# First attention stage: the norm behind the attention is applied on GpSimd, behind its spreading of k, instead of on VectorE

## The reference

```
x = x + attn(layernorm(x))       # once: windows of 64 tokens, 16 heads of 8
x = x + ffn_stack(layernorm(x))  # 6 layers: local attention (16 heads of 64,
                                 # windows of 32, rotary) and a gated feed-forward

# attn: qkv = xw @ W_qkv; q, k = layernorm over a head of 8, times gamma, plus beta
#       out = softmax(q k^T) v @ W_proj + b_proj
```

## Time and profile before

| what | value |
|---|---|
| runs of the kernel, us | 3247.95, 3230.7, 3246.5 (median 3246.5) |
| the profiled execution, us | 3239.37 |
| its span in the trace, us | 3237.6 |
| busy: PE, DVE, ACT, POOL | 96%, 86%, 79%, 82% |
| mean granted TensorE clock | 0.989 |
| the 32 executions of L366 on VectorE | 694 ns each on average, from 330 to 1353 |

### The profile page before, as it was taken

How to read it: one execution, slowest core, us unless ns; L and a number is a source line. 1 busy time by engine, 2 the same in 40 slices (tenths; PEclk the granted TensorE clock), 3 DMA queues, 4 the chain that set the end, 5 groups by cost and what they waited for, 6 DMA issues and landing times.

```text
span 3237.6 us, 123133 instructions
## 1 busy us (share of the span) xinstructions
PE 3121.0 (96%) x52802; PEld 2720.9 (84%) x52802; DVE 2769.2 (86%) x3716; ACT 2546.3 (79%) x3699; POOL 2647.6 (82%) x2646
## 2 busy tenths in 40 slices
PE   7988999999999999999999999999999999999997
PEld 4657888888888888888888888888888888888886
DVE  7978888888888888888888888888888888888884
ACT  5766788787878888787878877887878788878876
POOL 6758888887888888888888888887888888888873
PEclk9989999999999999999999999999999999999999
DMA  2001111111111111111111111111111111111111
GB/s 66 15 24 38 48 36 45 43 35 42 46 43 42 44 37 43 37 51 43 41 35 41 42 48 41 41 41 40 39 47 46 43 35 41 44 41 40 40 41 48
DMA packets 62044, 134.01 MB, mean 41 GB/s; under 512 B 11584, under 2 KB 35264, under 8 KB 61504
## 3 DMA queue, kind: packets, MB, share of 16 engines
q1 hardware_dynamic: 61504, 126.14, 13.5%
HBM read 21.27 MB, written 4.19 MB: 8 GB/s over the span
## 4 chain that ended last, share of the span: by engine, by line
PE 88%; ACT 2%; issue 2%; POOL 1%; DVE 0%; POOLq 0%; DVEq 0%
PE pair L215 71%; PE pair L218 17%; ACT qT L901 0%; ACT PT L882 0%; ACT X L920 0%; ACT X L906 0%; ACT sq L879 0%; ACT sq L891 0%; ACT VA L914 0%; ACT Sx L886 0%; POOL qk L1145 0%; POOL qk L1164 0%; DVE ss L1024 0%; DVE pair L1051 0%; DVE ts L1020 0%
## 5 line engine op out<-in xcount | busy, mean ns | idle before, releaser
L1164 POOL TENSOR_TENSOR qk<-qk,ts 128x1024 f32<-128x1024 f32 x384 | 910.5, 2383 | 70.5 <-DVE ts L1020 61.4
L1145 POOL TENSOR_TENSOR qk<-qk,rn 128x1024 f32<-128x1024 f32 x384 | 724.0, 1907 | 15.1
L1016 DVE TENSOR_TENSOR qk<-pair,tab 128x1024 f32<-128x1024 f32 x384 | 468.3, 1220 | 266.3 <-ACT sq L879 258.0
L879 ACT ACTIVATE sq<-pair 128x1024 f32<-128x1024 f32 x191 | 196.0, 1026 | 442.1 <-PE pair L215 441.9
L215 PE MATMUL pair<-wq_h,xs_h 128*128 128x512 f32 x1154 | 513.9, 445 | 2.5 <-issue 1.5
L1179 POOL TENSOR_TENSOR Sx<-Sx,rden 128x1024 f32<-128x1024 f32 x192 | 365.3, 1903 | 170.1 <-DVE rden L1096 170.1
L1020 DVE TENSOR_TENSOR ts<-pair,tab 128x1024 f32<-128x1024 f32 x384 | 466.4, 1215 | 0.0
L1024 DVE TENSOR_REDUCE ss<-sq 128x16 f32<-128x1024 f32 x384 | 464.3, 1209 | 0.0
L215 PE MATMUL pair<-wq_h,xs_l 128*128 128x512 f32 x1152 | 463.3, 402 | 0.1
L215 PE MATMUL pair<-wq_l,xs_h 128*128 128x512 f32 x1152 | 462.1, 401 | 0.6 <-issue 0.5
L218 PEld LDWEIGHTS pair<-small,qk 128*128 128x128 f32 x3072 | 350.2, 143 | 84.2 <-issue 53.0
(11 more groups left out here) (127 smaller groups left out, 6675.4 us busy)
## 6 DMA issues: line engine op xcount, KB each, us to landing
VB<-VA SPq DMA_DIRECT2D x192, 384.0 KB, 3.5
VB<-VA SPq DMA_DIRECT2D x96, 128.0 KB, 3.4
wq_raw<-wqkv SPq DMA_DIRECT2D x18, 512.0 KB, 5.1
xf<-xT SPq DMA_DIRECT2D x96, 64.0 KB, 1.9
xf<-xT SPq DMA_DIRECT2D x96, 63.8 KB, 2.0
wo_sb<-wo SPq DMA_DIRECT2D x6, 512.0 KB, 3.4
X<-x_in SPq DMA_DIRECT2D x4, 512.0 KB, 6.5
x_kept<-X SPq DMA_DIRECT2D x4, 512.0 KB, 2.7
```

Of the source, the lines that this page charges most:

```text
L879: A_.activation(sq[:, 0, :], one[:, :], ACT.Square).then_inc(S["squared"], 1)
L1016: V_.tensor_tensor(h3(qk[:, now, kind, :], DH), h3(source[:, :], DH), rep(factors[:, 2 * kind, b, :], HEADS, DH), ALU.mult)
L1145: G_.tensor_tensor(x, x, bc(rn[:, then, kind * HEADS:(kind + 1) * HEADS], HEADS, DH), ALU.mult).then_inc(S["scaled"], 1)
L1164: G_.tensor_tensor(qk[:, now, kind, :], qk[:, now, kind, :], ts[:, kind, :], ALU.add).then_inc(S["added"], 1)
```

## The change

GpSimd makes z in the same step as before, at the end of its own work on the tile pipeline, behind L406 and in front of the extra work of steps 8, 10 and 16 (step 4 comes before the first z). VectorE's instruction is gone. The operation, its operands and its semaphore `a_z` are the same. GpSimd now waits for its own `a_normed` before it, and for the transpose of z of two tiles ago. In the hand-over, the wait in front of `rest_of_x` is for z of tile 26 (step 34) in place of the spreading of the last tile.

```diff
@@ first_dve
-            i = s - 8
-            if tile(i):
-                if tile(i - 2):
-                    e.wait_ge(S["a_zT_done"], nth("a_zT_done", i - 2))
-                V_.tensor_scalar(z1[:, i % 2, :], X1[:, i, :], mv1[:, s % 2, 1, 0:1], rn1[:, s % 2, 2 * H1 + 1:2 * H1 + 2],
-                                 ALU.subtract, ALU.mult).then_inc(S["a_z"], 1)
@@ first_pool
                 last.then_inc(S["a_spread"], 1)
+            i = s - 8
+            if tile(i):
+                e.wait_ge(S["a_normed"], nth("a_normed", s))
+                if tile(i - 2):
+                    e.wait_ge(S["a_zT_done"], nth("a_zT_done", i - 2))
+                G_.tensor_scalar(z1[:, i % 2, :], X1[:, i, :], mv1[:, s % 2, 1, 0:1], rn1[:, s % 2, 2 * H1 + 1:2 * H1 + 2],
+                                 ALU.subtract, ALU.mult).then_inc(S["a_z"], 1)
 
             if s in (4, 10, 16):
@@ gpsimd
             first_stage(pool, first_pool, -1, TILES + 3)
-            pool.wait_ge(S["a_spread"], nth("a_spread", LAST))
+            pool.wait_ge(S["a_z"], nth("a_z", TILES + 2 - 8))
             rest_of_x(pool, first, 0)
```

## The result

The kernel with the change has a median of 3253.6 us (3238.9 to 3266.3, 16 runs), the kernel before one of 3246.3 us (3230.1 to 3255.4, 16 runs). The ratio is 1.0032, with a 95% interval of 1.0017 to 1.0047. By the ratio the change costs 5.5 to 15 us, most likely about 10 (the medians are 7.3 apart). The time lies inside the predicted range, but that range was 28 us wide, mostly for the spread between runs, so this says little. The loss lies inside the 0.5% called "same", but it is a loss, and about six times the 1.7 us of the forecast.

The account below looks back on a forecast made before the run. A first-stage ring over TensorE, ScalarE and GpSimd, not VectorE, was taken to set the step; 0 (regular steps) + 1.2 (steps 8, 10, 16) + 0.5 (hand-over) = +1.7 us, giving 3245 us, range 3230 to 3258.

Parts of the forecast that it names:

- the 0.5% called "same": Whole kernel: a change under about 0.5%, 16 us, counts as none; chances faster 0.03, same 0.92, slower 0.05.
- The regular steps cost and gain nothing: Steps 9, 11 to 15, 17 to 32: z hides in GpSimd's idle time, and VectorE's saving becomes waiting; cost and gain 0.
- the gap of 0.84: Regular steps: time z may take between GpSimd's spreading of k and L379 without moving anything; cover gone from 0.95.
- VectorE doesn't set the pace: Regular steps: TensorE releases VectorE; the rival that VectorE paces gave up to 10.8 us less, total 3234, chance 0.05.
- the ring over ScalarE and GpSimd: Regular step: closed chain of scores, transposes, L439, L445, L406 and scores again, taking 5.81 us, without VectorE.
- The head start of TensorE: Hand-over: last z earlier, block 1's transpose and projection 1.9 us earlier, lost in longer waits; worth 0. Rival keeping it: 0.05.
- z's price: z on GpSimd: 0.40 us, bounded by a scalar operation on 34 columns (0.227) and a same-size two-input operation (0.456).
- the prediction's 0.66: z on GpSimd at twice VectorE's 0.33, from the skill page; the sum would be 2.7 instead of 1.7 us.
- (b): Steps 8, 10 and 16, with other GpSimd work behind z: each z moves everything behind it, 3 x 0.40 = 1.2 us.
- (c): Hand-over: the last z, step 39, makes L1164 0.48 us later, and the chain behind it +0.5 us.
- a rival in the hand-over: Hand-over: TensorE's clock falls in a longer wait, two groups of eight transposes double, +2 us, total 3247; chance 0.2.
- slower: the operation is dear and outgrows the gap: Regular steps: z over 0.95 us lengthens 22 steps; chance 0.08, or 0.03 for 16 us or more (z = 1.43).

Follow-up runs that it names:

- the 28 steps without the four named: Whole kernel before, with z moved to GpSimd in all steps but 8, 10, 16 and 39: 3243.3 us against 3244.8, ratio 1.0001 [.9984, 1.0019].
- Its new order alone: One layer, kernel before with GpSimd's extra work spread, and VectorE dividing the attention's output ahead of the maxima: 773.2 us, ratio .2380 to the whole kernel before.
- the one-layer kernels: Kernels with one layer of the second stage instead of six, first stage and hand-over complete: before 773.2 us, after 784.5 us.
- The filled kernel: Changed kernel with one layer, TensorE repeating the products for v twice in steps 9, 11 and 17: 778.9 us, ratio .2402 to the whole kernel before.
- the last z alone: Kernel before with one layer, z moved to GpSimd only in step 39: 780.1 us, ratio .2409 to the whole kernel before.
- the projection done twice: One layer, z on GpSimd only in step 39, TensorE also making the k projection of block 1 twice: 778.7 us, ratio .2400 to the whole kernel before.
- the four z without the others: Kernel before with one layer, z moved to GpSimd only in steps 8, 10, 16 and 39: 786.9 us, ratio .2424 to the whole kernel before.
- the fastest version: Whole kernel before with GpSimd's extra work spread, new VectorE and ScalarE orders, z on GpSimd in steps without extra work: 3236.8 us, ratio .9975.

## Why the prediction was partly wrong

Right, step by step:
- *The regular steps cost and gain nothing.* 5.81 against 5.80, idle 0.79 in front of L296 (0.73 predicted), and the 28 steps without the four named give 1.0001 in the whole kernel. The argument from the earlier trace rows held. It held with little to spare, and by luck: the prediction counted on a z of 0.40, and one of 0.80 just fits the gap of 0.84. Up to 6 us there are not excluded.
- *VectorE doesn't set the pace.* Its new order alone left 5.81; with the ring over ScalarE and GpSimd shortened as well, the step fell to 5.70.
- *The loss lies in steps 8, 10, 16 and the hand-over, in full length.* The steps grew by 0.81, 0.81 and 0.79, where 0.4 was predicted.
- *The head start of TensorE is lost in the next wait* (3.54 for 1.48 in front of the transposes).

None of the prediction's signs of being wrong appeared (z over 0.95, a regular step under 5.75, L1176 not late): they guarded the gap and the pace, and not the terms that failed.

Wrong, first: **z's price**, 0.40 with bounds of 0.227 and 0.456. It measures 0.802. The upper bound was no bound: the row it came from has the size but not the form, and z's form costs more than an operation with two full inputs. With 0.802 the same sum gives 3 x 0.80 + 0.92 = 3.3 us, not 1.7. The Trainium skill, page "GPSIMD Engine Reference", section "Engine selection", speaks of about twice VectorE's time for two inputs, and of roughly line rate for one. z has one full input, so the prediction's 0.66 applied the factor of another case, and it was set aside for the row. Measured is 0.80 against VectorE's 0.33, a factor of 2.4: for this form the measurement and the page's word on one input differ, and the measurement decides; only the form with two constants, 0.30 us, is near VectorE's 0.33.

Wrong, second, and the larger part: **what follows a late chain.** The sum put it at nothing: the steps of (b) were priced at z alone, and (c) at z and its wait. TensorE's clock stood there only as a rival in the hand-over, at +2 and with a chance of 0.2. In the traces the step behind the late one also grows: 8.19 for 5.81 behind step 10, with the clock at 0.78 over the stretch, where the wait of TensorE in front had grown from 1.05 to 1.85 (5 of 6 such steps, 2.1 to 2.7 us each, against 5 of 14 at 1.3 to 1.4). And the hand-over's transposes are at half speed whenever the last z is GpSimd's (six of six, and none of eleven without), as that rival said; but in the changed kernel only the first group of eight doubles, by 0.87, and the second takes 1.07. That filling the wait takes the slow step behind steps 10 and 16 away is shown in one profile, its worth in time (5.2 us) only just.

The sum as it stands: 10.4 measured (5.5 to 15), 3.3 of it GpSimd's work on the chain, some 7 what follows. In the one-layer kernels 11.3 and 3.3, so 8.0.

Does the clock account for these 7 to 8? From run to run time and mean granted clock go together. In the 62 runs of the whole kernel before in the four batches, a run takes 2.5 us more for each 0.001 of clock less, with 2.8 us of scatter about this line. The 16 runs of the changed kernel have a mean clock of .9862 for .9881 and take 7.1 us more on average than those 62; 4.8 of it go with the clock, and 2.3 are left at equal clock. In the one-layer kernels it is 0.49 us for each 0.001, so the .960 for .972 goes with 5.6 of the 10.8 between the means, and 5.3 are left; the filled kernel, whose clock is that of before, lies 5.2 above it. These are estimates from runs of different batches and good to 1 or 2 us; within that, z's own 3.3 us and the slow stretches make up the loss. They say that the slow stretches and the time go together, and not why the clock falls.

How the slow part divides isn't settled. The filled kernel puts 5.2 behind steps 8, 10 and 16; the last z alone cost 8.1 with 0.9 of work, of which 2.9 may have gone away with the projection done twice; and the four z without the others cost 13.0. These add up to more than the whole, and each is good to about 3 us.

The rival "slower: the operation is dear and outgrows the gap" was right that it is dear (0.80 for 0.40), and wrong that it outgrows the gap: z stayed under 0.84.

## What to carry to other kernels

Price an operation by a row with its exact form, operators and operands, not by one of the same size: at 128 columns on GpSimd, two constants, two values for each partition and two full inputs took 0.30, 0.81 and 0.46 us, a factor of up to 2.7. If no row has the form, the range has no top.

Work that makes TensorE wait longer can cost more than its own length, because slow stretches followed the longer waits more often and lasted longer; count for each late chain how long TensorE stands in front of it. And freeing an engine that doesn't set the pace pays nothing until the ring that does is cut: z on GpSimd in every step lost 10 us alone. In the steps without extra work, and not in the last, it belongs to the fastest version once ScalarE's and VectorE's orders were changed and GpSimd's long steps were spread.

An effect of 0.3% in a long kernel wants the repeated part cut away: with five of six layers left out 11 us stood out of 775 in four runs a side, where 16 runs a side of the whole kernel just told the sign.

## What the runs showed of the hardware

- GpSimd's scalar operation on 128 columns: 0.30 us with two constants (multiply, add), 0.54 with one constant (multiply), 0.60 with one per-partition operand (multiply), 0.81 with two (subtract, multiply). The one with a single constant being dearer than that with two was not expected (one sample each; z itself is 0.802 over 32).
- The clock's half level came in stretches of about one step of the pipeline: behind waits of TensorE of 1.85 us in 5 of 6 cases, behind waits of 0.75 to 1.06 in 5 of 14, and in the drain with no pattern that these runs show (0.57 over ten us in the kernel before, 0.89 in the changed one).
- Behind a wait of 2.29 us the eight transposes ran at full speed in one kernel and behind one of 2.02 at half speed in another: the last wait alone doesn't tell.
